# Curvature stage: four channels in four partition groups, fields as 32x32 products of full float32 from turned copies of the image

## The chip, the cores and the metric

The kernel runs on one core of a Trainium2 chip, as one program. The metric is the device time of one execution in microseconds; of the kernel before there are three, and one more with the profiler on.

## The reference

The input is x[16, 16, 32, 32] (batch, channel, row, column). Four layers follow: a window and patch attention block with large weight matrices (L0), two blocks of two 3x3 convolutions with a ReLU and a residual (L1, L2), and ten steps of a curvature flow on every channel by itself (L3), which is what the change touches:

```
def step(u, _):
    ux, uy, uxx, uxy, uyy = _derivs(u)        # 3x3 Sobel filters, once or twice, clipped to +-10
    g2 = ux * ux + uy * uy
    denK = jnp.maximum(1.0 + g2, EPS)
    K = jnp.clip((uxx * uyy - uxy * uxy) / (denK * denK + EPS), -5.0, 5.0)
    denH = jnp.sqrt(1.0 + g2 + EPS)
    H = ((1.0 + uy * uy) * uxx - 2.0 * ux * uy * uxy + (1.0 + ux * ux) * uyy) / (2.0 * denH ** 3 + EPS)
    H = jnp.clip(H, -5.0, 5.0)
    diff = jnp.clip(alpha * K + beta * H, -1.0, 1.0)
    u = u + DT * diff
    u = jnp.pad(u[:, :, 1:-1, 1:-1], ((0, 0), (0, 0), (1, 1), (1, 1)), mode='edge')
    return (u, None)
u, _ = jax.lax.scan(step, x, None, length=10)
return 0.7 * u + 0.3 * x
```

## The kernel before

Five engines run five instruction streams that meet by semaphores; the order within each stream is written out by hand. For the first 400 us SP streams weight slots from memory into `ring`, and PE multiplies them against thin operands (`thin`, L397: 16 output slots at the end, four column strips of 32 columns side by side on 256 columns). The convolutions of L1 and L2 run between the slots in six waves of columns on the image `xa` (128 partitions are 8 rows x 16 channels; the free side is 4 row groups x 34 columns x 16 images), and the last wave stands behind the last slot (L531 to L538 on PE, L1020 on ACT, L822 on DVE).

Then comes the curvature stage. The 16 channels are four chunks of four. A chunk's image `u[c]` has on its 128 partitions 32 rows x 4 channels, on the free side 34 columns x 16 images = 544. It is gathered from `xa` by picking matmuls (`chunk_rows`, L545, in two parts, columns 0 to 23 and 24 to 31) that ACT (L1005, L1080) and DVE (L914) copy out of PSUM. A slot is one step of one chunk, 40 slots; chunk c comes round every fourth. In a slot k:

- PE (`fields`, L589) makes the five fields ux, uy, uyy, uxx, uxy on 480 columns. The vertical part of each filter is a 128x128 matrix of `vmats`, the horizontal part a shift of the columns: 2, 3, 5, 3 and 4 terms, 17 in all. The image stands as a high and a low part of the type float32r (`u_parts`; high by ACT, L1039, low by POOL, L1143), so each term is two matmuls, 34 in a slot. ux and uy go to two banks of one of two sets, uxy to a third of the set; uyy and uxx share banks 3 and 4 for all slots.
- DVE (`slot_step`) runs ten instructions: the clip of ux, uy (L870, of `fld1`), the update of u two slots back (L877, behind L867, which works in the bank of uxy), K and H of the slot before (L883), the clip of uyy, uxx (L888, of `fld2`), the clip of uxy (L891, of `fldxy`), then L894, L898, L903, L910 and, for the next slot, L867.
- ACT squares, logarithms and exponentials (L1046 to L1075); POOL products and sums (L1152 to L1170), and L1164, which copies the border columns of the updated image.

PE waits in a slot for ACT's high and POOL's low part, for K/H of two slots back, for the clip L888 of the slot before (banks 3 and 4), and before uxy for the update two slots back:

```
if reuse:
    te.wait_ge(ve["u"], k - 2)
stencil(bank[:, b1 + 2, :], u_hi[c], first, UXY, True)
stencil(bank[:, b1 + 2, :], u_lo[c], first, UXY, False).then_inc(pe["fldxy"], 1)
```

After slot 40 PE applies the edge rows (L636), DVE mixes with 0.3 x (`x3`, which ACT's L1085 made at the start), and SP stores five pieces.

## Time and profile before

| what | value |
|---|---|
| three runs | 753.15 us median, 752.92 to 755.58 |
| the profiled execution | 752.96 us, span 750.8 us |
| busy of the span | PE 662.3 us, DVE 439.6, ACT 373.8, POOL 324.6 |
| DMA | 166.54 MB, mean 222 GB/s over the span, over 400 GB/s in most of the first half |
| chain that ended last | DVE 38%, PE 28%, DMA 25%, issue 6% |

The page divides the span into 40 slices of 18.8 us. For the first 21 the DMA line reads 9, the weights come in; from the 24th on it reads 0, and PE, DVE and ACT read 9 until the last slice: that is the curvature stage. PE is busy in both, so the share of its busy time over the span says little of what bounds a stage. The granted clock of PE (PEclk) is given in tenths; 9 stands for 90% and over.

### The profile page before, as it was taken

How to read it: one execution, taken by the hardware profiler on the slowest of the kernel's cores; microseconds unless marked ns; L12 is line 12 of the kernel's file. 1: busy time of each engine (PE TensorE's matmuls, PEld its weight loads, DVE VectorE, ACT ScalarE, POOL GpSimd, SP SyncE). 2: the span in 40 equal slices, each digit the busy share in tenths (PEclk: the TensorE clock that was granted, in tenths of full speed). 3: DMA queues.
4: the chain of work that ended last, by engine and by line, in shares of the span. 5: the costliest groups of instructions: out<-in, count | busy, mean ns of one | idle time of the engine just before them, and what ended most of it. 6: DMA issues, size and time to landing. Idle time of an engine off the chain costs nothing.

```text
span 750.8 us, 11211 instructions
## 1 busy us (share of the span) xinstructions
PE 662.3 (88%) x4384; PEld 463.7 (62%) x4384; DVE 439.6 (59%) x660; ACT 373.8 (50%) x630; POOL 324.6 (43%) x311
## 2 busy tenths in 40 slices
PE   5997799998985565787999999999999999999994
PEld 3784585465442233444555687777778777787782
DVE  5630000086040212232344499999999999999997
ACT  1310000050000010111223599999999999999995
POOL 1000000010030600000000589999999999999993
PEclk9999799999995689999999999999999999999997
DMA  9999999999999999999993000000000000000001
GB/s 339 431 410 399 399 427 404 430 424 404 427 421 369 420 422 429 429 428 425 425 413 137 1 2 0 1 0 0 0 0 0 0 0 0 0 0 0 0 0 56
DMA packets 20946, 166.54 MB, mean 222 GB/s; under 512 B 1840, under 2 KB 2224, under 8 KB 11568
## 3 DMA queue, kind: packets, MB, share of 16 engines
q1 hardware_dynamic: 19552, 162.60, 52.5%
q0 software_dynamic: 688, 2.04, 0.8%
q10 hardware_dynamic: 672, 1.41, 0.5%
q8 instruction: 26, 0.43, 0.2%
q14 instruction: 8, 0.07, 0.0%
HBM read 164.99 MB, written 1.05 MB: 221 GB/s over the span
## 4 chain that ended last, share of the span: by engine, by line
DVE 38%; PE 28%; DMA 25%; issue 6%; ACT 1%; POOL 1%; DVEq 0%; POOLq 0%; SPq 0%; ACTq 0%
DMA ring<-wout_w 15%; PE bank L381 8%; PE bank L397 7%; DVE ring L883 6%; DVE ring L888 5%; DVE ring L870 4%; DVE bank L867 4%; DVE bank L903 4%; PE bank L505 4%; PE bank L450 4%; DMA ring<-wv_w 4%; DMA ring<-wqk_p 3%; DVE bank L891 3%; DVE ring L894 3%; DMA ring<-wout_p 3%
## 5 line engine op out<-in xcount | busy, mean ns | idle before, releaser
L589 PE MATMUL bank<-u_parts,vmr 128*128 128x480 f32 x1360 | 308.9, 384 | 6.5 <-DVE reg_a L877 4.3
L589 PEld LDWEIGHTS bank<-u_parts,vmr 128*128 128x128 f32 x1360 | 249.7, 188 | 65.6 <-DVE reg_a L877 16.6
L397 PE MATMUL bank<-ring,small 128*32 128x256 f32 x1152 | 77.3, 416 | 34.0 <-DMA ring<-wout_w 29.9
L397 PEld LDWEIGHTS bank<-ring,small 128*32 128x32 f32 x1152 | 38.6, 118 | 64.8 <-issue 26.6
L397 PE MATMUL bank<-ring,xw 128*32 128x256 f32 x1024 | 65.0, 414 | 15.1 <-DMA ring<-wv_w 15.1
L1101 POOL MEMSET reg_d<- 128x2176 f32 x1 | 1.9, 1911 | 150.9 <-PE bank L457 150.9
L718 DVE SCALAR_TENSOR_TENSOR reg_a<-bank,prm 128x512 f32<-128x512 f32 x4 | 2.8, 691 | 104.8 <-PE bank L457 104.8
L1129 POOL DMA_DIRECT2D vmr<-vmats x1 | 0.6, 566 | 145.2 <-PE bank L397 145.2
L381 PE MATMUL bank<-reg_a,ring 128*128 128x256 f32 x256 | 58.2, 390 | 5.3 <-DMA ring<-wqk_p 4.6
L397 PEld LDWEIGHTS bank<-ring,xw 128*32 128x32 f32 x1024 | 34.1, 118 | 43.9 <-DMA ring<-wv_w 19.1
L381 PEld LDWEIGHTS bank<-reg_a,ring 128*128 128x128 f32 x256 | 49.8, 196 | 14.0 <-DMA ring<-wqk_p 5.5
L1168 POOL TENSOR_TENSOR ring<-ring 128x480 f32<-128x480 f32 x40 | 49.2, 1231 | 9.8 <-ACT ring L1060 9.8
L1160 POOL TENSOR_TENSOR ring<-ring 128x480 f32<-128x480 f32 x40 | 48.9, 1224 | 8.7 <-DVE ring L888 5.8
L847 DVE STREAM_TRANSPOSE reg_b<-bank 128x256 f32<-128x256 f32 x16 | 7.2, 450 | 77.3 <-PE bank L397 77.3
L1152 POOL TENSOR_TENSOR ring<-ring 128x480 f32<-128x480 f32 x40 | 49.1, 1228 | 3.1
L1012 ACT ACTIVATE reg_e<-xa 32x288 f32<-32x288 f32 (+9 forms) x24 | 10.0, 415 | 81.2 <-DVE xa L851 42.0
L1170 POOL TENSOR_TENSOR ring<-ring 128x480 f32<-128x480 f32 x40 | 49.2, 1229 | 0.0
L1155 POOL TENSOR_TENSOR ring<-ring 128x480 f32<-128x480 f32 x40 | 48.9, 1222 | 0.0
L883 DVE TENSOR_TENSOR ring<-ring,bank 128x960 f32<-128x960 f32 x40 | 46.1, 1153 | 3.6 <-POOL ring L1152 2.0
L888 DVE TENSOR_SCALAR ring<-bank 128x960 f32<-128x960 f32 x40 | 46.0, 1150 | 2.2 <-PE bank L589 2.2
L870 DVE TENSOR_SCALAR ring<-bank 128x960 f32<-128x960 f32 x40 | 45.8, 1145 | 2.4 <-PE bank L589 2.4
L898 DVE SCALAR_TENSOR_TENSOR ring<-bank,ring 128x960 f32<-128x960 f32 x40 | 45.8, 1145 | 0.0
(195 smaller groups left out, 1019.7 us busy)
## 6 DMA issues: line engine op xcount, KB each, us to landing
ring<-wv_w SPq DMA_DIRECT2D x32, 2048.0 KB, 23.9
ring<-wout_w SPq DMA_DIRECT2D x30, 2048.0 KB, 37.0
ring<-wqk_p SPq DMA_DIRECT2D x4, 2048.0 KB, 21.1
ring<-wqk_w SPq DMA_DIRECT2D x4, 2048.0 KB, 19.5
ring<-wv_p SPq DMA_DIRECT2D x2, 2048.0 KB, 19.6
ring<-wout_p SPq DMA_DIRECT2D x2, 2048.0 KB, 22.9
ring<-wout_w SPq DMA_DIRECT2D x4, 1024.0 KB, 36.2
vmr<-vmats POOLq DMA_DIRECT2D x1, 1664.0 KB, 7.2
```

Source lines behind the costliest of these rows:

```text
L381: ins = te.matmul(bank[:, 4 + n % 2, (h % 2) * TOK:(h % 2 + 1) * TOK], half[2 * (k % NSLOT) + h // 4][:, c, h % 4 * DH:(h % 4 + 1) * DH], ...
L397: ins = te.matmul(bank[32 * j:32 * j + 32, b_, n0:n0 + 256], lhs(c), slot[k % NSLOT][:, c, 256 * j:256 * j + 256], start=start and c == 0, ...
L589: last = te.matmul(dst[:, 0:NF], mat(m, first), p3[:, 2 + off:S + off, :], start=(high and n == 0), stop=(not high and n == len(terms) - 1))
L870: v.tensor_scalar(two(f(q, 0, 2)), fields_in(q, 0, 2), 10.0, -10.0, ALU.min, ALU.max).then_inc(ve["clip1"], 1)
L883: v.tensor_tensor(two(kh[n]), two(num[n]), fields_in(n, 0, 2), ALU.mult).then_inc(ve["kh"], 1)
L888: v.tensor_scalar(two(f(q, 3, 2)), bank[:, 3:5, 0:NF], 10.0, -10.0, ALU.min, ALU.max).then_inc(ve["clip2"], 1)
L898: v.scalar_tensor_tensor(two(ab[q]), fields_in(q, 0, 2), 1.0, two(f(q, 3, 2)), ALU.add, ALU.mult).then_inc(ve["outer"], 1)
L1152: p.tensor_tensor(num[n][:, NF:2 * NF], abs_[n], cxy[n], ALU.add).then_inc(po["hn"], 1)
L1155: p.tensor_tensor(cxy[q], fld[q][:, 0:NF], fld[q][:, NF:2 * NF], ALU.mult).then_inc(po["cxy"], 1)
L1160: p.tensor_tensor(mxy[q], fld[q][:, 3 * NF:4 * NF], fld[q][:, 4 * NF:5 * NF], ALU.mult).then_inc(po["m"], 1)
L1168: p.tensor_tensor(num[q][:, 0:NF], mxy[q], sqm[q], ALU.subtract).then_inc(po["num"], 1)
L1170: p.tensor_tensor(abs_[q], ab[q][:, 0:NF], ab[q][:, NF:2 * NF], ALU.add).then_inc(po["absum"], 1)
```

## The change

The chunk's layout becomes four whole channels in four groups of 32 partitions, one row of the image to a partition. A vertical filter is then a 32x32 matrix (`vmats` is a quarter as wide and repeats for the four groups). Besides `u[c]` there are three turned copies, in which the four groups stand one, two and three groups further. `product` makes one term of one field as four 32x32 matmuls of full float32: output group j, and input group (j + t) % 4 of the copy turned by t. ux and uxx take t = 0, uy t = 1, uyy t = 2, uxy t = 3; the 17 terms of a slot are interleaved over the fields. The high and low parts, and what made them, are gone. PE now waits at the start of a slot for the clip L888 of the slot before, and for the update two slots back before the last eight products instead of the last field; its loop over the steps is written out. On DVE the update comes ahead of the clip of ux, uy.

The image gets into its new layout by DMAs on SP: `xa` to `image` in DRAM (8 DMAs a part), then from there the image and its turned copies (7 DMAs a chunk and part, 28 a part). In every later step SP makes the three turned copies of a chunk from `u[c]`, two DMAs each. ACT's copies for `x3` wait for these loads.

```diff
-NVM = 2 * len(MATS) * P
+NVM = 2 * len(MATS) * S
+TURNS = NCH - 1
+U_PIECES = 1 + 2 * TURNS
...
-        def mat(name, first):
+        def mat(name, first, quad):
             n = MATS.index(name) + (0 if first else len(MATS))
-            return vmr[:, n * P:(n + 1) * P]
+            return vm[quad * QUAD:(quad + 1) * QUAD, n * S:(n + 1) * S]
...
             sp.wait_ge(pe["slot_used"], U_ALL)
+            sp.dma_start(vm, vmats).then_inc(ld_vm, 16)
             sp.dma_start(edge_m, edge).then_inc(ld_edge, 16)
+            def pieces(t):
+                cut_ = QUAD * t
+                return [(cut_, P, 0)] + ([(0, cut_, P - cut_)] if t else [])
+            def move_image(half):
+                w0, w1 = early_columns(half)
+                to = image[half].rearrange("(c g r) n -> c g r n", c=C, g=G)
+                for r in range(RG):
+                    sp.dma_start(to[:, :, r, :], xa4[r * C:(r + 1) * C, :, 1 + w0:1 + w1, :]).then_inc(st_image[half], 16)
+                sp.wait_ge(st_image[half], 16 * RG)
+                for x in range(NCH):
+                    for t in range(NCH):
+                        whole = u[x] if t == 0 else turned[:, t - 1, x, :]
+                        for p0, p1, from_ in pieces(t):
+                            sp.dma_start(whole[p0:p1, (1 + w0) * B:(1 + w1) * B],
+                                         image[half][x * P + from_:x * P + from_ + p1 - p0, :]).then_inc(ld_u[x], 16)
+            sp.wait_ge(po["padz"], 3)
+            sp.wait_ge(ve["conv"], conv_done(WAVES - 2, NCONV - 1))
+            move_image(0)
+            sp.wait_ge(ve["conv"], conv_done(WAVES - 1, NCONV - 1))
+            move_image(1)
+            with sp.Fori(1, STEPS) as i:
+                for c in range(NCH):
+                    sp.wait_ge(po["pad"], i * NCH + (c + 1 - NCH))
+                    for t in range(1, NCH):
+                        for p0, p1, from_ in pieces(t):
+                            sp.dma_start(turned[p0:p1, t - 1, c, :], u[c][from_:from_ + p1 - p0, :]).then_inc(ld_turn[c], 16)
...
-            def chunk_rows(x, g, half):
-                w0, w1 = early_columns(half)
-                return te.matmul(bank[QUAD * g:QUAD * (g + 1), chunk_bank(x, half), chunk_cols(half)],
-                                 pick[:, x * QUAD:(x + 1) * QUAD],
-                                 xa4[:, g, 1 + w0:1 + w1, :], start=True, stop=True, skip_group_check=True)
-            def chunk_first(x):
-                te.wait_ge(ve["bank_turn"], NO + min(x, 2) + 1)
-                for g in range(G):
-                    ins = chunk_rows(x, g, 0)
-                ins.then_inc(pe["chunk"], 1)
...
-            def stencil(dst, part, first, terms, high):
-                p3 = part.rearrange("p (w b) -> p w b", b=B)
-                for n, (off, m) in enumerate(terms):
-                    last = te.matmul(dst[:, 0:NF], mat(m, first), p3[:, 2 + off:S + off, :],
-                                     start=(high and n == 0), stop=(not high and n == len(terms) - 1))
+            te.wait_ge(ve["conv"], conv_done(WAVES - 1, NCONV - 1))
+            def product(dst, c, t, first, terms, n):
+                off, m = terms[n]
+                image_ = (u[c] if t == 0 else turned[:, t - 1, c, :]).rearrange("p (w b) -> p w b", b=B)
+                for j in range(NCH):
+                    i_ = (j + t) % NCH
+                    at_ = slice(QUAD * i_, QUAD * (i_ + 1))
+                    last = te.matmul(dst[QUAD * j:QUAD * (j + 1), 0:NF], mat(m, first, i_), image_[at_, 2 + off:S + off, :],
+                                     start=(n == 0), stop=(n == len(terms) - 1), skip_group_check=True)
                 return last
-            def fields(k, c, first, reuse):
+            def fields(k, c, first, i):
                 b1 = bank_set((c + 1) % 2)
-                if first:
-                    te.wait_ge(po["lo_first"], c + 1)
-                if first and c == 1:
-                    te.wait_ge(ac["u_in"], NCH + 2)
-                    te.wait_ge(ve["u_in"], 2)
-                te.wait_ge(ac["hi"], k)
+                reuse = not first or c >= 2
+                ux, uy, uxy, uyy, uxx = (bank[:, n, :] for n in (b1, b1 + 1, b1 + 2, 3, 4))
                 if reuse:
                     te.wait_ge(ve["kh"], k - 2)
-                stencil(bank[:, b1, :], u_hi[c], first, UX, True)
-                te.wait_ge(po["lo"], k)
-                stencil(bank[:, b1, :], u_lo[c], first, UX, False)
-                stencil(bank[:, b1 + 1, :], u_hi[c], first, UY, True)
-                stencil(bank[:, b1 + 1, :], u_lo[c], first, UY, False).then_inc(pe["fld1"], 1)
-                if reuse or c:
+                if not first or c:
                     te.wait_ge(ve["clip2"], k - 1)
-                for n, terms in enumerate((UYY, UXX)):
-                    stencil(bank[:, 3 + n, :], u_hi[c], first, terms, True)
-                    ins = stencil(bank[:, 3 + n, :], u_lo[c], first, terms, False)
-                ins.then_inc(pe["fld2"], 1)
+                if not first:
+                    te.wait_ge(ld_turn[c], i * 16 * 2 * TURNS)
+                te.wait_ge(ld_u[c], 2 * 16 * U_PIECES)
+                for n in range(2):
+                    product(ux, c, 0, first, UX, n)
+                    product(uy, c, 1, first, UY, n)
+                    product(uyy, c, 2, first, UYY, n)
+                product(uxx, c, 0, first, UXX, 0)
+                product(uy, c, 1, first, UY, 2).then_inc(pe["fld1"], 1)
+                product(uyy, c, 2, first, UYY, 2)
                 if reuse:
                     te.wait_ge(ve["u"], k - 2)
-                stencil(bank[:, b1 + 2, :], u_hi[c], first, UXY, True)
-                stencil(bank[:, b1 + 2, :], u_lo[c], first, UXY, False).then_inc(pe["fldxy"], 1)
+                for n in range(2):
+                    product(uxx, c, 0, first, UXX, n + 1)
+                    ins = product(uyy, c, 2, first, UYY, n + 3)
+                    if n == 1:
+                        ins.then_inc(pe["fld2"], 1)
+                    product(uxy, c, 3, first, UXY, n)
+                product(uxy, c, 3, first, UXY, 2)
+                product(uxy, c, 3, first, UXY, 3).then_inc(pe["fldxy"], 1)
             te.wait_ge(ld_vm, 16)
-            te.wait_ge(ac["hi_first"], NCH)
             for c in range(NCH):
-                fields(c + 1, c, True, c >= 2)
-            with te.Fori(1, STEPS) as i:
+                fields(c + 1, c, True, None)
+            for i in range(1, STEPS):
                 for c in range(NCH):
-                    fields(i * NCH + (c + 1), c, False, True)
+                    fields(i * NCH + (c + 1), c, False, i)
...
-                if new:
-                    v.wait_ge(pe["fld1"], k)
-                    v.tensor_scalar(two(f(q, 0, 2)), fields_in(q, 0, 2), 10.0, -10.0, ALU.min, ALU.max).then_inc(ve["clip1"], 1)
...
                     inner = u[c][:, 2 * B:S * B]
                     v.scalar_tensor_tensor(inner, mixed(q), -DT, inner, ALU.max, ALU.add).then_inc(ve["u"], 1)
+                if new:
+                    v.wait_ge(pe["fld1"], k)
+                    v.tensor_scalar(two(f(q, 0, 2)), fields_in(q, 0, 2), 10.0, -10.0, ALU.min, ALU.max).then_inc(ve["clip1"], 1)
...
-            for x in range(1, NCH, 2):
-                v.wait_ge(pe["chunk"], NCH + x + 1)
-                v.tensor_copy(u_half(x, 1), bank[:, 4 + x, chunk_cols(1)]).then_inc(ve["u_in"], 1)
...
-            def high(k, c, later):
-                if not later:
-                    u_there(c)
-                    a.activation(u_hi[c][:, SECOND], u[c][:, SECOND], ACT.Copy).then_inc(ac["hi"], 1)
...
-                if c is not None:
-                    high(k + 2, c, True)
...
-            for x in range(2):
-                a.wait_ge(pe["chunk"], NCH + 2 * x + 1)
-                a.activation(u_half(2 * x, 1), bank[:, 4 + 2 * x, chunk_cols(1)], ACT.Copy).then_inc(ac["u_in"], 1)
-                high(x + 1, x, False)
-            for x in range(2, NCH):
-                high(x + 1, x, False)
             for x in range(NCH):
+                a.wait_ge(ld_u[x], 2 * 16 * U_PIECES)
                 a.activation(x3[:, x, :], u_in(x), ACT.Copy, scale=0.3).then_inc(ac["x3"], 1)
...
             p.wait_ge(pe["slot_used"], U_ALL)
-            p.dma_start(vmr[:, :], vmats).then_inc(ld_vm, 16)
+            p.memset(turned.rearrange("p t c (w b) -> p (t c) w b", b=B)[:, :, 0:S + 2:S + 1, :], 0.0).then_inc(po["padz"], 1)
...
-            def low(k, c, later=True):
-                p.wait_ge(ac["hi"], k)
-                at = slice(B, (S + 1) * B) if later else SECOND
-                p.tensor_tensor(u_lo[c][:, at], u[c][:, at], u_hi[c][:, at].bitcast(F32),
-                                ALU.subtract).then_inc(po["lo"], 1)
...
-    four = lambda m: np.kron(m.T, np.eye(CC))
-    mats = [four(op(n)[0] * op(n)[1]) for n in MATS] + [four(op(n)[0] * op(n)[1] @ edge) for n in MATS]
-    return (np.concatenate(mats, 1).astype(np.float32), four(edge).astype(np.float32))
+    mats = [(op(n)[0] * op(n)[1]).T for n in MATS] + [(op(n)[0] * op(n)[1] @ edge).T for n in MATS]
+    return (np.tile(np.concatenate(mats, 1), (NCH, 1)).astype(np.float32), np.kron(np.eye(CC), edge.T).astype(np.float32))
...
+    args.append([nc.dram_tensor(f"image{h}", (C * S, n * B), F32).ap() for h, n in enumerate((EARLY, S - EARLY))])
```

PE, the stage's slot for chunk 0. Before (`u_parts` are the high and low parts, `vmr` the matrices), from the slot's first matmul to the first of uxy, behind which 7 more follow:

```order
L589 MATMUL bank<-u_parts,vmr 128x480 [waits ve_kh]
L589 MATMUL bank<-u_parts,vmr 128x480
L589 MATMUL bank<-u_parts,vmr 128x480 [waits po_lo]
L589 MATMUL bank<-u_parts,vmr 128x480 x7
L589 MATMUL bank<-u_parts,vmr 128x480 [waits ve_clip2]
L589 MATMUL bank<-u_parts,vmr 128x480 x15
L589 MATMUL bank<-u_parts,vmr 128x480 [waits ve_u]
```

Now, from the wait for the update, where 9 of the 17 products are done, to the first matmul of the next slot (`reg_a` is the image, `ring` holds the turned copies; four matmuls are one product):

```order
L586 MATMUL bank<-reg_a,ring 32x480 [waits ve_u]
L586 MATMUL bank<-reg_a,ring 32x480 x3
L586 MATMUL bank<-ring 32x480 x8
L586 MATMUL bank<-reg_a,ring 32x480 x4
L586 MATMUL bank<-ring 32x480 x16
L586 MATMUL bank<-reg_a,ring 32x480 [waits ld_turn1,ld_u1,ve_clip2,ve_kh]
```

Of a slot's 34 matmuls 8 stood behind the wait for the update; of its 68 now 32 do, 8 products of four. The wait for ve_clip2 has moved from the middle of the slot to its start.

DVE, two neighbouring slots of the stage in the middle. Before:

```order
L867 TENSOR_SCALAR bank<-bank,small 128x480 [waits ve_diff]
L870 TENSOR_SCALAR ring<-bank 128x960 [waits pe_fld1]
L877 SCALAR_TENSOR_TENSOR reg_a<-bank,reg_a 128x480 [waits ac_x3,ve_clipd]
L883 TENSOR_TENSOR ring<-ring,bank 128x960 [waits ac_inv,po_hn,po_num]
L888 TENSOR_SCALAR ring<-bank 128x960 [waits pe_fld2]
L891 TENSOR_SCALAR bank<-bank 128x480 [waits pe_fldxy]
```

Now:

```order
L865 TENSOR_SCALAR bank<-bank,small 128x480 [waits ve_diff]
L872 SCALAR_TENSOR_TENSOR reg_a<-bank,reg_a 128x480 [waits ac_x3,ve_clipd]
L875 TENSOR_SCALAR ring<-bank 128x960 [waits pe_fld1]
L881 TENSOR_TENSOR ring<-ring,bank 128x960 [waits ac_inv,po_hn,po_num]
L886 TENSOR_SCALAR ring<-bank 128x960 [waits pe_fld2]
L889 TENSOR_SCALAR bank<-bank 128x480 [waits pe_fldxy]
```

The update (L877, now L872) stood behind the clip of ux and uy (L870, now L875), and now stands ahead of it, right behind the instruction that it waits for (L867, now L865).

SP behind the last weights. Before there was the load of `edge`, and then the stores of the result:

```order
L341 DMA ring<-wout_w 128x4096 x30
L346 DMA ring<-wout_w 128x2048 x4
L350 DMA ring<-edge 128x128
L356 DMA out<-ring 128x512 x3
L356 DMA out<-ring 128x256 x2
```

Now, down to the fifth of the seven loads of chunk 0's first part:

```order
L341 DMA ring<-vmats 128x832
L342 DMA ring<-edge 128x128
L354 DMA image<-xa 64x1x384 x8
L360 DMA reg_a<-image 128x384
L360 DMA ring<-image 96x384
L360 DMA ring<-image 32x384
L360 DMA ring<-image 64x384 x2
```

Two more loads, and seven for each of the other three chunks, make the 28 of the first part; then come 8 stores and 28 loads for the second part, the loop of the turned copies, and the stores of the result.

## Rows read from the trace of the kernel before

**Rows 1.** The page: span, and the clock granted to TensorE in 40 slices.
```profile
span 750.8 us, 11211 instructions
...
PEclk9999799999995689999999999999999999999997
```

**Rows 2.** Stretches A:B in us: length, busy PE, PEld, DVE, ACT, POOL, granted clock, DMA.
```profile
402.00:418.00 16.00, 15.35 (x76) 7.86 (x68) 7.60 (x20) 8.03 (x18) 2.60 (x3) 1.00 0.31 111
560.00:600.00 40.00, 39.13 (x174) 31.59 (x173) 39.77 (x52) 39.08 (x62) 38.10 (x37) 1.00 0.00 0
...
742.00:750.00 8.00, 1.94 (x4) 1.18 (x4) 4.72 (x13) 1.72 (x3) 0.00 (x0) 0.50 0.36 131
```

**Rows 3.** Timeline of DVE, one slot: start us, length us, engine, line.
```profile
600.74 0.66 DVE L891 TENSOR_SCALAR bank<-bank 128x480 f32<-128x480 f32 x1
...
604.12 0.72 DVE L867 TENSOR_SCALAR bank<-bank,small 128x480 f32<-128x480 f32 x1
...
605.81 0.64 DVE L877 SCALAR_TENSOR_TENSOR reg_a<-bank,reg_a 128x480 f32<-128x480 f32 x1
...
608.65 0.66 DVE L891 TENSOR_SCALAR bank<-bank 128x480 f32<-128x480 f32 x1
```

**Rows 4.** Timeline of PE and POOL in that slot.
```profile
606.51 7.74 PE L589 MATMUL bank<-u_parts,vmr 128*128 128x480 f32 x34 [0.17 <-DVE reg_a L877]
...
610.00 0.25 POOL L1164 TENSOR_TENSOR reg_a<-reg_a,ones 128x32 f32<-128x32 f32 x1
```

**Rows 5.** Groups by line from 440 us on: count, busy us, mean ns, idle before.
```profile
L589 PE MATMUL bank<-u_parts,vmr 128*128 128x480 f32 x1269 | 289.0, 385 | 6.3 <-DVE reg_a L877 4.3 <-DVE reg_g L877 1.0
...
L1143 POOL TENSOR_TENSOR u_parts<-reg_a,u_parts 128x512 fp32r<-128x512 f32 x27 | 35.4, 1310 | 0.0
```

**Rows 6.** Timeline of PE, output stage: matmuls in four column strips.
```profile
396.40 1.07 PE L397 MATMUL bank<-ring,small 128*32 128x256 f32 x16
...
399.39 2.80 PE L397 MATMUL bank<-ring,small 128*32 128x256 f32 x48
```

**Rows 7.** Timeline from the last convolution to the first curvature slot.
```profile
402.25 0.33 SPq L350 DMA_DIRECT2D ring<-edge  x1
...
417.64 0.75 DVE L822 SCALAR_TENSOR_TENSOR xa<-bank,prm,xa 128x512 f32<-128x512 f32 x1 [2.01 <-PE bank L538]
...
419.79 20.72 PE L589 MATMUL bank<-u_parts,vmr 128*128 128x480 f32 x94 [0.18 <-ACT u_parts L1035]
...
422.39 1.16 DVE L870 TENSOR_SCALAR ring<-bank 128x960 f32<-128x960 f32 x1 [2.42 <-PE bank L589]
...
423.64 0.61 ACT L1046 ACTIVATE ring<-ring 128x480 f32<-128x480 f32 x1 [1.11 <-DVE ring L870]
...
427.50 0.67 DVE L891 TENSOR_SCALAR bank<-bank 128x480 f32<-128x480 f32 x1 [0.56 <-PE bank L589]
428.07 0.65 DVE L894 SCALAR_TENSOR_TENSOR ring<-bank,ring 128x480 f32<-128x480 f32 x1
...
432.73 1.15 DVE L883 TENSOR_TENSOR ring<-ring,bank 128x960 f32<-128x960 f32 x1 [1.32 <-POOL ring L1152]
```

**Rows 8.** Timeline of DVE, last slots.
```profile
732.82 1.15 DVE L883 TENSOR_TENSOR ring<-ring,bank 128x960 f32<-128x960 f32 x1
...
744.60 0.73 DVE L867 TENSOR_SCALAR bank<-bank,small 128x480 f32<-128x480 f32 x1
745.36 0.66 DVE L877 SCALAR_TENSOR_TENSOR reg_g<-bank,reg_g 128x480 f32<-128x480 f32 x1
```

**Rows 9.** Timeline of SP's DMA issues at the start.
```profile
0.74 0.39 SPq L317 DMA_DIRECT2D reg_a<-x_patch  x1
1.19 0.42 SPq L318 DMA_DIRECT2D xw<-x_window  x1
```

**Rows 10.** DMA issues by line: count, KB each, median us to landing.
```profile
out<-ring SPq DMA_DIRECT2D x3, 256.0 KB, 2.1
...
ring<-edge SPq DMA_DIRECT2D x1, 64.0 KB, 1.8
```

99 lines of the change are left out of this document (20 added, 79 removed).

## The prediction

> **What bounds the kernel now.** I read the page first, then stretches, then the timeline of one slot, then the seam between the last convolution and the first slot, and last the end. The page's profiled execution has a span of 750.8 us and took 752.96 us [rows 1]; the sum below is made against 752.96, which stands 0.2 us under the median of the three runs, 753.15.
>
> The curvature stage is 40 slots (10 steps of 4 chunks). The gradient product K/H, DVE's L883, first starts at 432.73 [rows 7] and for the 39th time at 732.82 [rows 8]: 300.09 us over 38 slots, 7.90 us each. In the middle DVE is busy for 39.77 of 40 us and PE for 39.13 [rows 2]. The timeline says which of the two it is: DVE's ten instructions follow each other from one L891 (600.74) to the next (608.65), 7.91 us, with no idle noted [rows 3]. PE's 34 passes of a slot take 7.74 us, and it then sits for 0.17 us until DVE's L877 releases it [rows 4]. So both are full, and DVE by a hair more. PE's 40 slots of passes are what the change goes at; DVE's ten instructions it leaves as they are. **No saving on PE can bring a slot under DVE's 7.9 us.**
>
> **What is removed.** PE's 34 full passes a slot, at 289.0/1269 = 0.228 us each [rows 5]; ACT's L1039; POOL's L1143, 1.31 us a slot [rows 5]; the gather of chunks by matmuls at L545. ACT and POOL set no end in a slot: DVE has no idle time that they ended [rows 3]. I price their removal at 0. What hides them is DVE's own work, and it stays.
>
> **What PE does instead.** 17 products a slot, each of four 32x32 matmuls on 480 columns. A full float32 matmul stands as two passes in the trace: a quarter of the last output slot, 8 matmuls in the code, is x16. The nearest row for tiles side by side is that stage, four column strips: 16 passes took 1.07 us and 48 took 2.80 [rows 6], so 32 more cost 1.73 us, or 0.216 us for four passes (one a strip) on 256 columns. Scaled to 480 columns a pass is 0.216 x 480/256 = 0.405 us, and a product whose four tiles run together 0.81 us. If nothing else overlapped, 17 products would be 13.8 us; if products on different tiles run beside each other, they stand in seven rounds: ux, uy and uyy twice, uxx, uy and uyy once, uxx, uyy and uxy twice, then uxy alone twice: 7 x 0.81 = 5.7 us. No row shows row groups side by side; the ends are 5.7 and 13.8 (and more, below). I take 5.7, since the strips, the nearest row, overlap without loss, and the tiles of the three products have no row-column pair in common.
>
> **The wait that appears.** 5.7 us is under 7.9, but PE is not free to place it. uxy goes to the bank that DVE uses as scratch until L877 (the update of u) two slots on, so PE waits for that update inside each slot, and the wait stands before all of the last eight products. Before, that was 8 passes of 0.228, and the clip of the mixed field (L891) came after K/H and L888. Now four uxy products go through the same four tiles one after another. The loop, in a slot:
> - DVE from L891 to L867: 604.12 - 600.74 = 3.38 us [rows 3];
> - L867 to the update, now right behind it and waiting for it: 745.36 - 744.60 = 0.76 [rows 8], where it was one instruction further;
> - the update to the start of PE: 606.51 - 605.81 = 0.70 [rows 3, 4];
> - eight passes on one tile: 7 steps of 0.405 = 2.84;
> - from the start of the last pass to DVE: ten passes and the release took 422.39 - 419.79 = 2.60 [rows 7], less 9 x 0.228 leaves 0.55; a pass of 0.4 instead of 0.2 adds 0.18: 0.73.
>
> Sum 8.41 us. DVE's own round, with L870 moved behind the update, I leave at 7.9, at most 0.1 more: an instruction that need not wait starts by 0.1 before the one ahead of it ends (L891 lasts 0.67 and L894 follows after 0.57 [rows 7]), and one that waits for it does not; that is under the loop either way. So each slot costs 8.41 - 7.90 = 0.51 us more, and DVE sits idle for it before L891. The first slot interval has no such wait to pay (PE is early there), the other 37 have: **+18.9 us**. Late next, if that wait went, is DVE itself.
>
> **The turned copies.** Six DMAs a chunk and step on SP. Their price in issue is between 0.33 us (the length of one [rows 7]) and 0.45 (the spacing of two [rows 9]); I take 0.40. To landing it is 1.8 to 2.1 us [rows 10]; 2.0. The border copy of a chunk ends at 610.25, 1.6 us after L891 starts [rows 3, 4], and the fields that need it begin as L888 of the next slot ends: 8.4 - 1.6 = 6.8 us later. Six issues and a landing are 4.4. Cost 0, cover 2.4 us; it is gone when an issue costs 0.8.
>
> **The seam.** This is the second term. Now SP moves the image, all of it in one queue: behind the last release (402.25 [rows 7]) two loads of matrices, 8 stores, their landing, 28 loads; then for the second part again 8 stores and a landing, and 7 loads until chunk 0 is whole. That is 53 issues and three landings: 402.25 + 53 x 0.40 + 3 x 2.0 = 429.45 for PE's first matmul, which was at 419.79 [rows 7]. The last convolution ends at 418.39 [rows 7] and is not what it waits for (SP reaches that point at 419.45). Then ACT: its copies for the final mix wait for all four chunks before its first square. Chunk 3 lands 21 issues later, 437.85; one copy of about 0.62 and two squares of 0.61 [rows 7] and about 1.0 put L894 at 440.1, and from L894 to K/H it is 432.73 - 428.07 = 4.66 [rows 7]: 444.7 against 432.73, **+12.0 us**. By the issue price the ends are +8.3 (0.33: then the convolution's end bounds the second part) and +15.7 (0.45). PE has then been idle for over 10 us. At the end of the run, after idle stretches, its granted clock is 0.50, 1.2 GHz, against 1.00 before [rows 2], so I expect the first slot's passes near 0.81 us. Three rounds at that, four at full clock and 0.6 to the release are 8.7, and from L891 to K/H it is 432.73 - 427.50 = 5.23 [rows 7]: 443.4, hidden by ACT's wait; with all seven at half clock it would be 446.6, 1.9 more, which the range holds.
>
> Sum: 752.96 + 12.0 + 18.9 = **784 us**. The end of the run (edge matmuls, stores) stays.
>
> **A rule against it.** The thin rows show four strips of one product written side by side into one bank, four partition groups apart [rows 6]. The Trainium skill, TensorEngine Tiling (Array Packing), Gotcha 1: PSUM Pressure, says that different row tiles cannot access the same bank simultaneously. In this change the four tiles of a product are four row groups and write one bank. No row here shows that form; by that rule the sum would be the second rival's, by the strips it is mine.
>
> **Rivals.**
> 1. *The wait is hidden* (chance 0.12). If PE's last rounds are shorter than scaled, or the release quicker, by 0.5 us, slots stay at 7.9 and the seam alone is paid: 765 us, 761 with the cheap seam. For it: the margin is small. Against: every term of the loop is a row.
> 2. *The four tiles of a product run one after another* (0.08). Then four uxy products are 16 x 0.81 = 13.0 us where I have 3.24: loop 18.1, +10.2 a slot, 37 times 10.2 + 12: about 1,143 us. For it: no row with row groups. Against: the strips. This is the case in which the rule above holds.
> 3. *Only two products at a time* (0.12). Five rounds behind the update, not four: loop 9.22, 37 x 1.32 + 12: 814 us.
> 4. *The clock falls* (0.05). PE is busy for some 5.7 of 8.4 us; at half clock eight passes cost 3.24 more, 37 x 3.75 + 12: about 904. Against: no half clock in the middle of the stage so far [rows 1], though at a fuller load.
> 5. *It comes out faster* (0.02). DVE's steps would have to be longer than need be because POOL and ACT share memory with it; POOL loses its longest operation. It decides from the point where a slot is under 7.90 - (12.0 + 3.8)/38 = 7.48 us; at 7.40 the kernel takes 746. Against: L891 takes 0.67 us in the first slot, where POOL and ACT are mostly idle, and 0.66 in the middle [rows 3, 7], so company does not lengthen DVE's work.
>
> A measurement of this kernel can tell about 0.5% (3.8 us) from no change. Within it: 0.03, if both seam and loop are much smaller. The forecast keeps 0.58. Slower by more: 0.58 + 0.12 + 0.08 + 0.12 + 0.05 = 0.95. The range 762 to 822 takes in my sum with its ends, most of the first rival and the third, about 0.8.
>
> **What would show it.** Right: a gap of near 0.5 us on DVE before each clip of the mixed field, ended by PE; passes on one tile 0.405 us apart and three products beside each other; PE idle for over 2 us in each slot until the update; first matmul near 429 with SP's queue full from 402; slots of 8.4. Wrong: slots of 7.9 without the gap (rival 1), a gap before the first two clips as well (rivals 2 and 3), a granted clock under 1.00 in the stage, or turned loads ending PE's wait.

## The result, and the profile after

The changed kernel takes **864.28 us** (median of 4 runs, 863.83 to 865.9) where the kernel before takes 753.24: a ratio of 1.147, 95% interval 1.1443 to 1.1498. The forecast was 784 us with a range of 762 to 822: slower, as forecast, but by 111 us in place of 31. The other 80 us went where the sum has nothing or too little. The profiled execution took 865.9 us with a span of 863.8, 113.0 more than before [rows 1]. The page, span and granted clock:

```profile
span 863.8 us, 19405 instructions
...
PE   6996999989565678798365777777667777777764
...
PEclk9996999999868989999878888888888888888886
...
L586 PE MATMUL bank<-reg_a,ring 32*32 32x480 f32 x1200 | 166.3, 659 | 101.7 <-DVE reg_a L872 50.3
...
L889 DVE TENSOR_SCALAR bank<-bank 128x480 f32<-128x480 f32 x40 | 26.7, 666 | 49.6 <-PE bank L586 49.6
```

In the curvature stage neither PE nor DVE is full any more, and PEclk stands at 8 where it was 9 [rows 1]. PE waits for the update (L872; L877 before), DVE for the clip of the mixed derivative (L889; L891 before). A slot on DVE, which answers to [rows 3], and PE in it:

```profile
641.08 1.16 DVE L886 TENSOR_SCALAR ring<-bank 128x960 f32<-128x960 f32 x1 [0.82 <-PE bank L586]
643.56 0.67 DVE L889 TENSOR_SCALAR bank<-bank 128x480 f32<-128x480 f32 x1 [1.33 <-PE bank L586]
...
646.95 0.72 DVE L865 TENSOR_SCALAR bank<-bank,small 128x480 f32<-128x480 f32 x1
647.71 0.66 DVE L872 SCALAR_TENSOR_TENSOR reg_a<-bank,reg_a 128x480 f32<-128x480 f32 x1
...
651.32 1.16 DVE L886 TENSOR_SCALAR ring<-bank 128x960 f32<-128x960 f32 x1 [0.82 <-PE bank L586]
```

```profile
648.42 0.60 PE L586 MATMUL bank<-reg_a,ring 32*32 32x480 f32 x4 [2.79 <-DVE reg_a L872]
...
648.85 0.58 PE L586 MATMUL bank<-reg_a,ring 32*32 32x480 f32 x4
...
649.25 0.89 PE L586 MATMUL bank<-reg_a,ring 32*32 32x480 f32 x4
...
649.90 1.04 PE L586 MATMUL bank<-reg_a,ring 32*32 32x480 f32 x4
```

From one L886 to the next it is 651.32 - 641.08 = 10.24 us. PE idles for 2.79 us until the update and starts again with passes 0.43 and 0.40 us apart; then one of 0.65, and the rest are 0.80 apart. Stretches around that point (columns as in [rows 2]) show what happened:

```profile
642.70:649.30 6.60, 3.81 (x109) 1.83 (x88) 5.70 (x8) 4.17 (x7) 4.61 (x5) 1.00 0.47 129
...
649.50:652.70 3.20, 3.20 (x42) 1.05 (x45) 2.15 (x2) 3.11 (x5) 1.35 (x2) 0.50 0.00 0
...
480.00:720.00 240.00, 173.06 (x3186) 74.70 (x3174) 189.89 (x238) 177.64 (x259) 146.46 (x143) 0.84 0.32 84
```

The clock is full (1.00) up to 649.3 and half (0.50, 1.2 GHz) from 649.5 to 652.7, just where most of the eight products lie for which DVE waits. Later slots show the same, with a mean clock of 0.84 from 480 to 720 us. It began with the third slot, where PE had idled for 2.24 us and its passes were 0.56 us apart soon after its return; a slot later the idle stretch was 2.79:

```profile
474.65 0.60 PE L586 MATMUL bank<-reg_g,ring 32*32 32x480 f32 x4 [2.24 <-DVE reg_a L872]
...
475.08 0.80 PE L586 MATMUL bank<-reg_g,ring 32*32 32x480 f32 x4
...
475.64 1.04 PE L586 MATMUL bank<-reg_g,ring 32*32 32x480 f32 x4
...
484.83 0.60 PE L586 MATMUL bank<-reg_a,ring 32*32 32x480 f32 x4 [2.79 <-DVE reg_a L872]
```

**Where the 113.0 us are.** The first K/H (L881) starts at 459.06, before at 432.73 [rows 7]: 26.3 us. The 39th starts at 843.91, so 38 slots took 384.85 us against 300.09 [rows 7, 8]: 84.8 us, 10.13 each on average. The end is 863.8 - 843.91 = 19.9 against 750.8 - 732.82 = 18.0: 1.9 us. The seam, on SP's queue, ACT and DVE:

```profile
405.11 0.33 SPq L341 DMA_DIRECT2D ring<-vmats  x1
...
406.03 5.13 SPq L354 DMA_DIRECT2D image<-xa  x8
...
413.24 0.34 SPq L360 DMA_DIRECT2D reg_a<-image  x1
...
427.73 5.04 SPq L354 DMA_DIRECT2D image<-xa  x8
434.21 0.34 SPq L360 DMA_DIRECT2D reg_a<-image  x1
...
439.26 0.63 ACT L1044 ACTIVATE ring<-reg_a 128x512 f32<-128x512 f32 x1 [21.56 <-DMA ring<-image]
...
452.46 0.63 ACT L1044 ACTIVATE ring<-reg_g 128x512 f32<-128x512 f32 x1 [4.26 <-DMA ring<-image]
453.00 0.59 ACT L1012 ACTIVATE ring<-ring 128x480 f32<-128x480 f32 x1
...
459.06 1.16 DVE L881 TENSOR_TENSOR ring<-ring,bank 128x960 f32<-128x960 f32 x1 [1.23 <-ACT bank L1039]
...
843.91 1.14 DVE L881 TENSOR_TENSOR ring<-ring,bank 128x960 f32<-128x960 f32 x1
```

Eight stores take 5.13 us to issue, 0.64 each; 28 loads from 413.24 to 427.7, 0.52 each. ACT copies the fourth chunk only at 452.46, and its first square stands behind that.

### The profile page after: what moved, and what is told of

Read it like the earlier page. It is cut to its first block, busy times and chain, and to the rows that moved or that the text cites. A ratio compares the mean times of both kernels' runs of the same rounds, so it can differ in the third digit from the quotient of the medians.

```text
span 863.8 us, 19405 instructions
## 1 busy us (share of the span) xinstructions
PE 650.6 (75%) x8400; PEld 344.9 (40%) x8400; DVE 446.5 (52%) x658; ACT 363.7 (42%) x580; POOL 270.7 (31%) x266
## 4 chain that ended last, share of the span: by engine, by line
PE 44%; DMA 25%; DVE 20%; issue 5%; SPq 4%; ACT 1%; POOL 0%; DVEq 0%; POOLq 0%; ACTq 0%
PE bank L586 24%; DMA ring<-wout_w 13%; PE bank L404 5%; PE bank L420 5%; PE bank L473 3%; PE bank L528 3%; SPq L360 3%; DVE bank L901 3%; DVE bank L889 3%; DVE bank L865 3%; DMA ring<-wv_p 3%; DMA ring<-wqk_p 3%; DMA ring<-wv_w 3%; DMA ring<-wout_p 3%; DVE ring L892 2%
## 5 line engine op out<-in xcount | busy, mean ns | idle before, releaser
L586 PE MATMUL bank<-ring 32*32 32x480 f32 x3840 | 297.6, 683 | 0.0
L586 PE MATMUL bank<-reg_a,ring 32*32 32x480 f32 x1200 | 166.3, 659 | 101.7 <-DVE reg_a L872 50.3
L586 PEld LDWEIGHTS bank<-ring 32*32 32x32 f32 x3840 | 105.9, 121 | 73.9 <-issue 66.2
L586 PEld LDWEIGHTS bank<-reg_a,ring 32*32 32x32 f32 x1200 | 44.4, 112 | 172.0 <-issue 68.6
L586 PE MATMUL bank<-reg_g,ring 32*32 32x480 f32 x400 | 55.1, 653 | 27.4 <-DVE reg_a L872 27.4
L1099 POOL TENSOR_TENSOR ring<-ring 128x480 f32<-128x480 f32 x40 | 48.5, 1212 | 73.5 <-DVE ring L875 73.5
L1102 POOL TENSOR_TENSOR ring<-ring 128x480 f32<-128x480 f32 x40 | 48.4, 1211 | 71.0 <-DVE ring L886 71.0
L1110 POOL TENSOR_TENSOR ring<-ring 128x480 f32<-128x480 f32 x40 | 48.5, 1212 | 52.8 <-ACT ring L1026 52.8
L886 DVE TENSOR_SCALAR ring<-bank 128x960 f32<-128x960 f32 x40 | 46.3, 1158 | 31.5 <-PE bank L586 31.5
L875 DVE TENSOR_SCALAR ring<-bank 128x960 f32<-128x960 f32 x40 | 45.9, 1148 | 23.6 <-PE bank L586 23.6
L889 DVE TENSOR_SCALAR bank<-bank 128x480 f32<-128x480 f32 x40 | 26.7, 666 | 49.6 <-PE bank L586 49.6
L1096 POOL TENSOR_TENSOR ring<-ring 128x480 f32<-128x480 f32 x40 | 48.1, 1202 | 3.1
L1112 POOL TENSOR_TENSOR ring<-ring 128x480 f32<-128x480 f32 x40 | 48.2, 1204 | 0.0
```

The lines of the kernel that those rows point to most:

```text
L586: last = te.matmul(dst[QUAD * j:QUAD * (j + 1), 0:NF], mat(m, first, i_), image_[at_, 2 + off:S + off, :], start=(n == 0), stop=(n == len( ...
L875: v.tensor_scalar(two(f(q, 0, 2)), fields_in(q, 0, 2), 10.0, -10.0, ALU.min, ALU.max).then_inc(ve["clip1"], 1)
L886: v.tensor_scalar(two(f(q, 3, 2)), bank[:, 3:5, 0:NF], 10.0, -10.0, ALU.min, ALU.max).then_inc(ve["clip2"], 1)
L889: v.tensor_scalar(mixed(q), mixed(q), 10.0, -10.0, ALU.min, ALU.max).then_inc(ve["clipxy"], 1)
L1096: p.tensor_tensor(num[n][:, NF:2 * NF], abs_[n], cxy[n], ALU.add).then_inc(po["hn"], 1)
L1099: p.tensor_tensor(cxy[q], fld[q][:, 0:NF], fld[q][:, NF:2 * NF], ALU.mult).then_inc(po["cxy"], 1)
```

## The experiments

There are two theories for the 80 us that the forecast lacked. **Idle clock:** the loop of waits (update, mixed derivative, its clip, update) is right, but it leaves PE idle in one long stretch a slot, and the half clock that follows lies on the loop itself. **Other cause:** the four-tile products take the clock down by themselves, or DVE is slowed by something. Each ratio is against the kernel before, timed beside that run on the same chip (752.6 to 754.3 us).

### More work for PE

```
-                product(uyy, c, 2, first, UYY, 2)
+                product(uyy, c, 2, first, UYY, 2); [product(uxx, c, 0, first, UXX, 0) for _ in range(2 if reuse else 0)]
```

> The changed kernel with two more copies of one product of 16 small matmuls each (uxx, first term, again from its start: the real one still comes last, so no result changes) where PE waits for the update. The loop of waits is left in. If PE's idle time of 2.8 us in a slot of 10.24 us is what takes the clock down, the granted clock stays at full for more of the time and the slot goes to 8.4 to 9.2 us, the time to 795 to 825 us although PE is given more to do. If the clock follows the work (more matmuls, lower clock), the slot grows to 10.5 to 11.5 us and the time to 875 to 910 us.

> As the kernel with two filling products, with three (2.4 us more at the full clock, about all of PE's idle time). If idle time takes the clock down: granted clock 0.97 or more in the steady stage, slot 8.4 to 8.8 us, time 795 to 810 us. If work takes it down: time 885 to 930 us.

> The changed kernel with one filling product of 16 small matmuls (0.8 us more PE work at the full clock, 1.6 at half) in place of two: the dose between none (864.28 us) and two (806.05 us). If idle time of PE takes the clock down by steps, the result lies between the two: some slots of 8.61 us, some with a stretch at half clock, granted clock 0.90 to 0.97 in the steady stage, time 815 to 850 us. If one product is already enough, 804 to 807 us; if it is worth nothing, 862 to 870 us.

(A product is four tiles of two passes, 8 matmuls in the rows, not 16; its time was as stated.) Measured: one filling product **804.48 us** (ratio 1.0678, 1.0653 to 1.0702), two **806.05** (1.0699, 1.0679 to 1.0718), three **807.3** (1.071, 1.0684 to 1.0736). 0.8 us more work for PE in each slot took 60 us off. The kernel with one, 480 to 560 us, and PE's start after the update:

```profile
480.00:560.00 80.00, 61.52 (x1318) 27.15 (x1320) 74.90 (x95) 69.33 (x102) 58.35 (x57) 1.00 0.39 103
```

```profile
637.33 0.60 PE L586 MATMUL bank<-reg_a,ring 32*32 32x480 f32 x4 [1.85 <-DVE reg_a L872]
```

The clock is full, PE's idle stretch 1.85 us, and the slot 8.61 us, the same with one, two and three. The other cause falls: with more small products the clock rises, and DVE's instructions have the lengths that they had. One was enough, the second case of its expectation.

The kernel with two filling products shows what the half clock costs on the loop, PE's start after the update and DVE's clip of the mixed derivative:

```profile
644.73 0.60 PE L586 MATMUL bank<-reg_g,ring 32*32 32x480 f32 x4 [1.05 <-DVE reg_a L872]
...
648.49 0.67 DVE L889 TENSOR_SCALAR bank<-bank 128x480 f32<-128x480 f32 x1 [0.52 <-PE bank L586]
```

From the one to the other it is 3.76 us. In the changed kernel PE starts at 648.42 and that clip, one slot of 10.24 us after 643.56, at 653.80: 5.38 us. The difference of 1.62 us is the whole difference between the two slots (10.24 - 8.61 = 1.63).

### The loop at full clock

Both on the kernel with two filling products, so that the clock stays out of it. First DVE's order as it was before the change (clip1, L875, ahead of the update), then one step the other way:

```
-                    v.wait_ge(pe["fldxy"], k)
-                    v.tensor_scalar(mixed(q), mixed(q), 10.0, -10.0, ALU.min, ALU.max).then_inc(ve["clipxy"], 1)
                     v.wait_ge(ac["sqr"], k)
                     v.scalar_tensor_tensor(slope[q], fields_in(q, 1)[:, 0, :], 1.0, p2[q],
                                            ALU.add, ALU.add).then_inc(ve["slope"], 1)
+                    v.wait_ge(pe["fldxy"], k)
+                    v.tensor_scalar(mixed(q), mixed(q), 10.0, -10.0, ALU.min, ALU.max).then_inc(ve["clipxy"], 1)
```

> On the kernel with two filling products (806.05 us, slot 8.61 us at full clock): DVE's order as it was before the change, clip1 ahead of the update. My theory says the slot is the loop update, mixed derivative, its clip, and so on: clip1's step of 1.07 us then lies in the loop once more, slot 9.68 us, 38 slots x 1.07 = 41 us, time 845 to 850 us if the clock stays full, more (860 to 890 us) if PE's longer idle time takes the clock down again. The rival that DVE or ACT as a whole sets the slot, whatever the order, says 806 us and no change.

> On the kernel with two filling products: the slope formula, which doesn't read the mixed derivative, goes ahead of its clip on DVE, so 0.57 us of DVE work covers what is left of PE's time in the loop (DVE idles 0.52 us there in each slot). The loop of waits predicts a slot of 8.09 us and 38 x 0.52 = 20 us less: 784 to 790 us. If ACT, with its 7.6 us of work in a slot and the squares of the mixed derivative now later, is what binds, the slot stays at 8.4 to 8.6 us and the time at 798 to 806 us.

Measured: **865.13 us** with the old order, **787.17** with the slope ahead. With the old order K/H starts come 9.54 us apart in some slots (the clock is 1.00 from 650.2 to 659.7, one of them) and 11.1 in the others (0.85 from 639.3 to 650.1); the clock from 480 to 720 us is 0.92. So the order that the change chose is worth 0.9 us a slot at full clock, and its absence lengthens PE's idle stretch to as much as 2.41 us and brings the half clock back. With the slope ahead the slot is 8.05 us and DVE full:

```profile
560.00:600.00 40.00, 38.19 (x768) 16.45 (x760) 39.79 (x51) 36.60 (x56) 31.14 (x30) 1.00 0.40 107
```

DVE's wait before the clip was 0.52 us in the kernel with fillers, and it is what went: (8.61 - 8.05) x 38 = 21 us against 18.9 measured. ACT did not bind.

### Taking the loop out

```
-                mixed = lambda s_: fields_in(s_, 2)[:, 0, :]
+                mixed = lambda s_: mx[s_]
-                if reuse:
+                if False:
                     te.wait_ge(ve["u"], k - 2)
```

(mx is a new tile in SBUF. The clip copies the field from the bank into it, after the update of two slots before; the rest of DVE's and ACT's work on the mixed field and on the update goes there.)

> The changed kernel with its loop of waits cut: the step's scratch (ends, diff, clipd) moves from the bank of the mixed derivative into an SBUF tile, so PE no longer waits for the update of two slots before. If the loop (update, then the mixed derivative of the slot after, then its clip) sets the slot and the half clock is what its idle time costs, the slot goes from 10.24 us to 7.6 to 8.4 us and the time to 775 to 800 us. If the half clock has another cause than the idle time of PE (the four small products themselves, or power), the rounds stay at 3 x 3.41 us in part and the time stays above 840 us. If DVE's own work were the bound, the slot would stay where it is as well, with DVE busy for all of it.

Measured: **878.75 us** (ratio 1.1657, 1.1635 to 1.168), slower than any theory had it. PE's wait was gone, but DVE was busy for all of the slot, now of 10.55 us, with instructions that had grown longer. Timeline of DVE and POOL:

```profile
639.87 1.21 POOL L1110 TENSOR_TENSOR ring<-ring 128x480 f32<-128x480 f32 x1 [0.59 <-ACT ring L1026]
639.89 1.70 DVE L901 SCALAR_TENSOR_TENSOR ring<-ring,small 128x480 f32<-128x480 f32 x1
641.03 1.63 POOL L1112 TENSOR_TENSOR ring<-ring 128x480 f32<-128x480 f32 x1
641.51 1.67 DVE L908 SCALAR_TENSOR_TENSOR ring<-ring 128x480 f32<-128x480 f32 x1
643.33 1.29 POOL L1096 TENSOR_TENSOR ring<-ring 128x480 f32<-128x480 f32 x1 [0.66 <-DVE ring L908]
643.60 1.53 DVE L872 SCALAR_TENSOR_TENSOR reg_a<-ring,reg_a 128x480 f32<-128x480 f32 x1
```

The difference (L901), the cross term (L908) and the update (L872) took 0.71, 0.65 and 0.66 us with one operand in a bank; with both in SBUF they take 1.70, 1.67 and 1.53, 2.9 us more a slot. Each ends 0.51 us after the POOL instruction beside it (641.08 and 641.59; 642.66 and 643.18; 644.62 and 645.13). So the bank as scratch, which makes the loop, is also what keeps DVE fast, and this run says nothing on the loop. It does show the half clock once more, away from the loop: PE idled for 2.67 and 2.83 us in two slots, until DVE's clip of uyy and uxx (L886), and the clock from 480 to 720 us was 0.85. Since DVE was busy for 239.21 of those 240 us, that cost nothing.

### The order without fillers

> The changed kernel without any filling product, DVE's slope ahead of the clip of the mixed derivative. At a constant full clock that was worth 19 us. Here the loop gains the same 0.57 us of slack; if the clock still falls in each slot, since PE idles longer than its work lasts, only part of it shows: slot 9.6 to 10.24 us, time 840 to 864 us. If the shorter slot itself keeps PE busy enough for the full clock, the slot is 8.05 to 8.4 us and the time 785 to 800 us.

The changed kernel with nothing but the slope ahead of the clip: **783.14 us** (ratio 1.0398, 1.0379 to 1.0418). One DVE instruction, moved by one place, takes 81 us off. The second branch of the expectation holds, with the time 2 us under its range:

```profile
480.00:560.00 80.00, 64.92 (x1360) 28.09 (x1360) 79.61 (x100) 73.31 (x110) 61.77 (x60) 1.00 0.39 105
```

```profile
633.19 0.60 PE L586 MATMUL bank<-reg_g,ring 32*32 32x480 f32 x4 [1.67 <-DVE reg_a L872]
```

Slot 8.05 us, clock 1.00, DVE full. If 19 us of the 81 are the loop's, as with the fillers, the other 62 are the clock's.

### Less work for PE

Does the sum of PE's idle time decide, or how it lies? Three runs on that last kernel leave products out of the computation: the third term of the mixed derivative; instead of it the round ahead of the wait (first term of uxx, third of uy and uyy; the signal for the clip of ux and uy then comes with the second term of uy); and both.

```
-                product(uxy, c, 3, first, UXY, 2)
```
```
-                product(uxx, c, 0, first, UXX, 0)
-                product(uy, c, 1, first, UY, 2).then_inc(pe["fld1"], 1)
-                product(uyy, c, 2, first, UYY, 2)
```

> The kernel with the slope ahead of the clip and no filling product (783.14 us, clock full, slot 8.05 us), with one product of the mixed derivative left out of the computation (its third term): PE has 0.8 us less to do in a slot and idles some 2.0 us in place of 1.2. If the clock follows PE's idle time, the granted clock falls to half in part of the steady stage, and the kernel that does less takes as long or longer: 785 to 850 us. If the clock does not follow idle time, nothing else can grow: DVE is busy for all of the slot, and the time stays at 781 to 784 us.

> The kernel with the slope ahead of the clip and no filling product, with the three products of one round left out of the computation (first term of uxx, third of uy and of uyy), which run ahead of PE's wait for the update. PE has 0.8 us less to do, as with one product of the mixed derivative left out, but its idle time is one stretch of some 2.4 us instead of 1.62 and 0.42. If one long stretch takes the clock down, the granted clock of the steady stage is 0.83 to 0.95 and the time 785 to 850 us for less work. If only the sum of idle time counts, clock and time stay as with the one product: 1.00 and 780 us.

> The same with the third product of the mixed derivative left out as well: the stretch of some 2.4 us stays, a shorter one of 0.4 to 0.8 us comes with it, sum about 2.8 us, as in the changed kernel. If the stretch alone decides, it behaves as the kernel without that last omission. If the sum decides, this one falls to half clock in part (clock 0.83 to 0.95) and the other doesn't. If neither falls, idle time at this slot length is not what does it, and the slot's length or the overlap of three products has to be looked at: both 778 to 781 us.

Measured: **780.17**, **823.47** and **799.71 us**. The three in this order, PE's starts after a wait:

```profile
632.91 0.60 PE L586 MATMUL bank<-reg_g,ring 32*32 32x480 f32 x4 [1.62 <-DVE reg_a L871]
...
636.25 0.60 PE L586 MATMUL bank<-reg_a,ring 32*32 32x480 f32 x4 [0.43 <-DVE ring L885]
```

```profile
526.43 0.61 PE L586 MATMUL bank<-reg_a,ring 32*32 32x480 f32 x4 [2.61 <-DVE reg_g L871]
...
536.05 0.60 PE L586 MATMUL bank<-reg_a,ring 32*32 32x480 f32 x4 [3.03 <-DVE reg_a L871]
```

```profile
522.16 0.60 PE L586 MATMUL bank<-reg_a,ring 32*32 32x480 f32 x4 [2.56 <-DVE reg_g L870]
...
525.50 0.60 PE L586 MATMUL bank<-reg_a,ring 32*32 32x480 f32 x4 [0.42 <-DVE ring L884]
```

And each one's stretch from 480 to 720 us:

```profile
480.00:720.00 240.00, 178.50 (x3840) 75.00 (x3840) 238.97 (x301) 221.09 (x331) 186.65 (x181) 1.00 0.41 107
```

```profile
480.00:720.00 240.00, 163.64 (x2950) 63.38 (x2960) 212.15 (x264) 195.77 (x290) 164.26 (x159) 0.88 0.36 94
```

```profile
480.00:720.00 240.00, 159.52 (x2968) 55.52 (x2968) 227.94 (x286) 211.20 (x314) 177.09 (x171) 0.92 0.39 102
```

With 1.62 and 0.43 us idle a slot the clock stays full, and the first expectation, that it would fall, was wrong. (In 7 of the 30 slots a turned copy's load ended PE's wait at the start of a slot, up to 1.15 us; no slot grew by it, as DVE was busy for 238.97 of the 240 us.) With one round left out ahead of the wait instead, the stretch is 2.61 us (the expectation put it at 2.4), the clock 0.88, and a kernel that does less than the one with the slope ahead takes 40 us longer. So work taken out ahead of the wait, where it lengthens the stretch, brings the half clock, and the same 0.8 us of PE's time taken out behind it does not. The pair differs in one more thing: a round is three products side by side, the other run leaves out one. The number of products alone does not order the runs either: the third has the fewest and yet a higher clock than the second. It also has the larger sum of idle time (2.98 us), so the sum alone does not order them; nor did it behave as the second, which the stretch alone had asked for. Which measure of PE's work or idleness counts stays open.

The same on the kernel before (the low parts of uyy and uxx left out, 26 passes a slot in place of 34):

> The kernel before with the low part of uyy and uxx left out of the computation (26 matmuls in a slot in place of 34). If PE's time was hidden behind DVE in the kernel before (DVE busy for all of a slot of 7.90 us), the time stays at 750 to 755 us: that is all the gain that fewer PE cycles could give there. If PE was the bound, 8 x 0.216 us a slot would come off, 40 slots, about 69 us. If the clock follows PE's busy share, it may fall instead and the time rise above 760 us.

Measured: **759.8 us**, ratio 1.007 (1.0045 to 1.0095).

```profile
480.00:720.00 240.00, 191.20 (x765) 154.37 (x765) 232.73 (x296) 230.50 (x355) 221.63 (x207) 0.92 0.00 0
...
616.02 0.67 DVE L890 TENSOR_SCALAR bank<-bank 128x480 f32<-128x480 f32 x1 [0.80 <-PE bank L589]
```

A quarter of PE's passes less and 5.5 us more: the clock fell to 0.92 and DVE is no longer full. Its rounds tell the two apart. The one from the clip of the mixed derivative (L890) at 599.46 to the next took 7.82 us, with PE's 26 passes in 5.9 us and DVE never waiting; the next, whose passes took 7.5 us, was 8.74 with the wait of 0.80 in the line above. So at full clock PE's passes were worth 0.08 us a slot, some 3 us in all (an estimate), and the half clock took that back and more.

### The seam, and all together

Both on the kernel with two filling products: ACT's queue stores the image's second half and loads it for chunks 1 and 3; and each chunk's copy on ACT comes after that chunk's squares.

```
-            move_image(1)
+            sp.wait_ge(st_image[1], 16 * RG)
+            load_image(1, (0, 2))
...
+                a.dma_start(to[:, :, r, :], xa4[r * C:(r + 1) * C, :, 1 + w0:1 + w1, :]).then_inc(st_image[1], 16)
```
```
+                if k <= NCH:
+                    mix(k - 1)
```

> On the kernel with two filling products: the second half of the image is stored by ACT's queue (8 DMAs), and its loads for chunks 1 and 3 issue there too; SP has those of chunks 0 and 2. If the seam is bound by SP's issuing one DMA after the other (0.64 us a store, 0.52 us a load), the stores of the second half start at 418.7 in place of 425.3 us, the first product 5 to 6 us earlier and the first K/H 10 to 14 us earlier, as ACT waits for the last chunk: time 792 to 801 us. If the DMA engines themselves or the round trip through DRAM bind, two queues only share them, and the time stays at 804 to 806 us.

> On the kernel with two filling products: ACT copies each chunk's image (x3) after the squares of that chunk rather than all four first. The first squares then wait for chunk 0 alone and start at 442.8 in place of 450.1 us, but the slots behind are held by the loads of their chunks (3.6 to 4.8 us each, less than a slot), so about 5 to 7 us should go: time 799 to 801 us. If the loads of the later chunks bind instead, 0 to 2 us go: 804 to 806 us.

Measured: **793.21** and **797.8 us**, 12.8 and 8.3 less than 806.05; the second is 1.2 us under its range. With two queues:

```profile
420.29 5.24 ACTq L1053 DMA_DIRECT2D image<-xa  x8
427.73 0.37 ACTq L1060 DMA_DIRECT2D reg_a<-image  x1
427.77 0.34 SPq L365 DMA_DIRECT2D reg_a<-image  x1
...
446.14 1.16 DVE L887 TENSOR_TENSOR ring<-ring,bank 128x960 f32<-128x960 f32 x1 [1.27 <-POOL ring L1116]
```

The two queues issue beside each other at little loss: ACT's eight stores take 5.24 us, its last six loads 3.17 and SP's beside them 3.12, though six of SP's loads beside the stores took 3.79. K/H starts at 446.14. What bound the seam was one queue's issue, and behind it ACT's wait for the last chunk.

> Two filling products, slope ahead of the clip, the image's second half over both queues, and each chunk's copy after its squares: all that helped so far. The parts add up if the causes are apart: 806.05 - 18.9 (slope) - 12.8 (queues) - 0 to 3 (copies, most of whose gain the queues already took) = 771 to 775 us, slot 8.05 us with DVE busy for all of it. That stays above the kernel before (753.8 us): 38 slots x 0.15 us, a seam some 11 us longer and an end 2 us longer. If the parts overlap (the last chunk's loads bind in both), 776 to 782 us.

> The same with one filling product. PE then has about 6.6 us of work in a slot of 8.05 us (0.82) where it has 7.4 (0.92) with two. If the full clock needs no more than this, the time is 771 to 775 us as with two; if PE's idle time of 1.4 us a slot still takes the clock down at times, 776 to 800 us.

> No filling product; slope ahead of the clip, the image's second half over both queues, each chunk's copy after its squares. From the kernel with the slope alone (783.14 us) the seam's mends take the 12.8 us that the queues gave and up to 2 us for the copies: 768 to 771 us, 1 to 3 us under the same with one or two filling products, whose PE work can still be late in single slots. If PE's idle time of 1.2 us a slot takes the clock down once the first slots come differently, 780 us or more.

Measured with two, one and no filling product: **773.51**, **772.03** and **771.31 us** (the last with ratio 1.0243, 1.0223 to 1.0262, and 0.3 over its range). The parts add up: 783.14 - 771.31 = 11.8 where the queues alone gave 12.8. The best is still 18 us over the kernel before, and its trace says where: the first K/H starts at 444.68, 12.0 later than in the kernel before, and the 39th at 750.43, 38 slots of 8.05 us with DVE busy for nearly all of each (5.7 more), the end is 0.3 longer. DVE bounds its slots as it bounded those of the kernel before, so nothing that PE does can shorten them.

```profile
560.00:640.00 80.00, 64.43 (x1362) 28.08 (x1360) 79.57 (x100) 73.21 (x111) 61.90 (x60) 1.00 0.40 107
```

## Why the prediction was wrong

- **DVE bounds the kernel before, so PE's saving brings nothing: right.** The run with a quarter of the passes left out gained nothing; its rounds at full clock were 7.82 us against 7.90.
- **The products: right.** Passes on one tile are 0.40 us apart and three products run beside each other (12 matmuls in each 0.40 at 466.5 and 648.5). The four row tiles of a product write one bank at once, 4 of the 12 matmuls in each 0.40, without loss, so rival 2 and the rule of the Trainium skill behind it (TensorEngine Tiling (Array Packing), Gotcha 1: PSUM Pressure) do not hold for this form; nor does rival 3.
- **The loop of waits: right in place, 0.2 us short.** The sum has 8.41 us; at full clock it is 8.61. L889 to L865 is 3.39 (3.38 forecast), L865 to the update 0.76 (0.76), the update to PE 0.71 (0.70). PE's start to the clip is 3.76 with the fillers (644.73 to 648.49) where I had 2.84 + 0.73 = 3.57; the seven steps of 0.40 account for 2.8, so it is the last pass and its release that I had some 0.2 too short. The first interval was 7.98, as said.
- **The clock: the step that failed.** The sum priced the eight passes on one tile behind the update at full clock (7 steps of 0.405 = 2.84 us), with no term for what PE's idle time ahead of them does to the clock. Rival 4 had that, at a chance of 0.05 and 904 us, as a clock that is half for all of the loop's passes. I wrote "no half clock in the middle of the stage so far, though at a fuller load" and let the first half of the sentence count. The same text has PE idle for over 2 us a slot among the signs that it is right, and reads from the end of the run that the clock is half after idle stretches; the two belonged together. What the runs showed: at a slot of 8.54 PE idled for 2.24 us, the clock fell within a microsecond of its return, most of the loop's passes took twice as long (PE's start to the clip 5.38 us in place of 3.76), so DVE was later, so the next stretch was 2.79. The loop feeds itself, until a third of each slot is at half clock: 10.24 us. Price: 864.28 - 804.48 = 59.8 us, and about 62 by the pair of runs with the slope. The Trainium skill (TensorE: Matmul & The Clock Gate, A second HAM failure mode: psum-queue depth-cycling) tells of a kernel whose short idle times between groups of matmuls make the clock swing; this trace agrees (stretches of 2.79 us, clock 1.00 and 0.50 in one slot).
- **The seam: +26.3 where I had +12.0.** The mechanism (SP's issues in one row, then ACT's wait for chunk 3) was right, the price of an issue was not: 0.40 was taken, 0.45 was the bound, and it was 0.64 for a store and 0.52 for a load, of shapes that no row of the kernel before shows. 53 issues cost 29.1 in place of 21.2 us (+7.9), their three landings 5.2 in place of 6.0 (-0.8). Chunk 3's copy came 13.2 after chunk 0's where I had 8.4 (+4.8). Another 2.9 is not the change's: SP was released at 405.1 in this profile, at 402.3 before, and at 401.8 to 404.3 in those of the other changed kernels. From chunk 3's copy to K/H it was 6.6 in place of 6.9. The first passes were 0.80 us apart, as said, and hidden by ACT's wait.
- **The turned copies: right for this kernel, with less in hand than I had.** From the second slot on no wait of PE was ended by one of their loads. But six issues took 3.72 us (0.62 each, where I had 0.40) and a landing 2.1 to 2.6, so the cover of 2.4 us was 1 us or less; in slots of 8.05 us they did end waits of PE, 6 times in the kernel with the slope ahead (0.9 us at most), and DVE's work hid them.

At full clock the time lies in the range, but not for the sum's reasons alone: with one filling product (804.48 us) the trace is 52.1 us longer than before, 25.2 in the seam, 26.6 in the 38 slots and 0.3 at the end, where the sum had 12.0 and 18.9. The range missed for the clock, which had been given 0.05; the seam and the loop were each too cheap besides.
